# Attention and a 4-bit linear layer on one core: queue points of four loads, a third place for values, two subtractions on another engine, one fill later

## The chip, the cores and the metric

The kernel runs on one core of a Trainium2 chip. The time is what the device takes for one launch, in microseconds (us): a median of separate runs. TensorE (PE) multiplies matrices, VectorE (DVE) and ScalarE (ACT) work element by element, GpSimd (POOL) too, SyncE (SP) only issues DMA transfers, all into one queue. Engines run their own instructions in order and wait for each other by semaphores.

## The reference

```python
x = layernorm(x + attention(x))        # x: 4 x 1024 x 512, f32
x = layernorm(x + linear(x))           # both operands rounded to 4 bits in blocks of 32
# attention: 32 heads of 16
q, k, v = x @ Wq.T, x @ Wk.T, x @ Wv.T
q1, q2 = halves(q); q = concat(q1*cos - q2*sin, q1*sin + q2*cos)   # k likewise (rope)
s = q @ k.T / 4 + bias[i - j]          # bias where 0 <= i - j < 256; masked where i < j
m = max(max_j(s), off);  p = exp(s - m)
out = (p @ v) / (sum_j p + exp(off - m)) @ Wo.T
```

## The kernel before

The work has three stages. Stage one (to about 326 us) makes q, k and v for 4096 tokens in 8 chunks of 512 tokens. Each chunk has four *pairs* (32 in all, numbered by `done` or `n`; b is the batch, eight pairs each). A pair is two 128-row tiles of q or k (the two halves that rope mixes) and one tile of v. f32 operands are split into a high and a low part: ScalarE writes the high part (`weight_hi`, `operand_hi`), VectorE the low part of the weights (L1291), GpSimd the low part of x (`operand_lo`, L1205). TensorE multiplies three products of 512 columns for each of four k-steps (L808).

For a pair, in order: ScalarE copies the two tiles out of PSUM (`take_up`, L980); VectorE multiplies them by the cosines (`by_cosine`, L1384) while GpSimd multiplies the copy by the sines (`turn_by_sine`, L1200); VectorE adds and subtracts (`rotate`, L1396). The result is cut into three bf16 parts: first part on ScalarE (L997), the rest on VectorE (`take_rest`, L1402), second part on ScalarE (`second_part`, L1001), third part on VectorE (`third_part`, L1371). The buffer `rest` is single: the next `take_rest` waits for the third part. SP stores the parts to DRAM (`store_parts`, six transfers), from four buffers, two of them for the last eight pairs. Values go from PSUM to one of two places in `v_sb` (L989), and from there to DRAM (L618); the last eight pairs use one place, since the other receives the first values for stage two.

The rope tables for cosines and sines hold two pieces, for even and odd pairs, and are reloaded by SP once in a chunk each (`load_rope`, L513). After batches 0, 1 and 2 SP also loads back the *stack* of that batch (`load_stack`, L540 and L543, nine transfers of 1.5 MB together): six blocks of q parts beside six of k parts, so that one bf16 matmul gives an accurate product.

From pair 12 on TensorE also computes the row maxima products of the first two batches between its product matmuls (`maxima`, L716), into a ring of three PSUM banks, and VectorE reduces them (`max_unit`, L1306 and L1313) at set places between a pair's steps. TensorE waits when all three banks are full.

Stage two (to about 1425 us) runs 8 groups of heads over 4 batches: scores, exponentials, products with v. Stage three is the output projection, the layer norms and the linear layer. The passage from stage one to stage two is called the seam here: the last pair's parts are made while the first score units run (`u` numbers them; ScalarE's exponentials are L1051), and three maxima units (`seam`) are done by VectorE in it.

SP's order in one step of stage one is: wait for the pair's values and store them; at the second pair of a chunk load the next x; at a chunk's last and first pair load a rope table; store the parts of the pair before; then `loads_beside`, the stack and bias loads. At the very start SP loads Wq and x in quarters (L516, L508), Wv (L519), the rope tables and, once VectorE has split Wq, Wk (L524). GpSimd fills some constants first, among them 3 rows of ones in the stacks (L1185) and the ones beside the values (L1188). ScalarE's first instruction waits for both kinds of fill (`ones_set`).

## Time and profile before

| | |
|---|---|
| runs | 1656.5, 1656.63, 1661.16 us; median 1656.63 |
| the profiled execution | 1662.25 us, span of its instructions 1660.3 us |
| granted TensorE clock, mean | 0.976 |
| busy: PE, DVE, ACT, POOL | 1555.8, 1291.1, 1108.2, 248.7 us |

A clock of 1.00 is 2.4 GHz, 0.50 is 1.2 GHz. "Idle before" in a row is the time that the engine stood still just before the instruction, and the name behind the arrow is what ended it. "issue" there means that the profile shows no releaser.

### The profile page before, as it was taken

The numbers are of one execution on the slowest core, as the hardware profiler recorded it, in microseconds if no ns is written. First come the engines' busy times: TensorE is split into PE (matmuls) and PEld (weight loads), VectorE is DVE, ScalarE is ACT, GpSimd is POOL, SyncE is SP. The second block draws the span as 40 slices with busy tenths as digits, with TensorE's granted clock in tenths as the row PEclk, the third lists the DMA queues.
The fourth block names the chain that finished last, engine by engine and source line by source line (L and its number), as shares of the span: only waits on it lengthen the run. The fifth ranks groups of instructions, "written<-read, shape, count | busy, mean of one in ns | idle before, by whom it ended". The sixth has DMA issues, their size and how long they took to land. (4 is left out here: it accounts for less than half of the span.)

```text
span 1660.3 us, 28811 instructions
## 1 busy us (share of the span) xinstructions
PE 1555.8 (94%) x9552; PEld 816.4 (49%) x9552; DVE 1291.1 (78%) x3830; ACT 1108.2 (67%) x1620; POOL 248.7 (15%) x157
## 2 busy tenths in 40 slices
PE   7999989789999999999999999999999998899984
PEld 5876657544444444444444444444444443444431
DVE  5567878678888888888888888878888876289995
ACT  4543434467787878878788787887778888434542
POOL 5544434200000000000000000000000000033442
PEclk9999999989999999999999999999999999999995
DMA  5595656534433334432542434433353202013221
GB/s 196 174 240 173 161 165 176 155 78 94 74 55 80 52 60 73 90 46 47 107 69 46 81 55 73 89 57 47 59 110 54 46 9 85 26 51 102 77 77 51
DMA packets 129257, 147.59 MB, mean 89 GB/s; under 512 B 48595, under 2 KB 81427, under 8 KB 129110
## 3 DMA queue, kind: packets, MB, share of 16 engines
q1 hardware_dynamic: 129110, 145.76, 39.4%
q8 instruction: 77, 1.26, 0.3%
q14 instruction: 70, 0.57, 0.1%
HBM read 102.32 MB, written 42.60 MB: 87 GB/s over the span
## 5 line engine op out<-in xcount | busy, mean ns | idle before, releaser
L1051 ACT ACTIVATE probs<-ps 128x1024 f32<-128x1024 f32 (+3 forms) x768 | 592.2, 810 | 181.5 <-PE ps L743 120.4
L1313 DVE CUSTOM_DVE_ANT_0 junk<-ps,bias_q 128x384 bf16<-128x384 f32 (+2 forms) x1024 | 502.7, 502 | 149.1 <-PE ps L716 135.3
L716 PE MATMUL ps<-k_stack,q_stack 96*128 96x384 bf16 (+3 forms) x1536 | 494.1, 335 | 24.0 <-DVE mx L1306 11.8
L737 PE MATMUL ps<-q_stack,k_stack 99*128 99x512 bf16 (+3 forms) x1536 | 490.5, 329 | 15.6 <-ACT ps L1066 5.3
L1306 DVE TENSOR_REDUCE mx<-ps 128x1 f32<-128x128 f32 (+3 forms) x768 | 365.3, 485 | 47.6 <-PE ps L716 40.6
L743 PE MATMUL ps<-bias_r,ident_r 128*128 128x384 f32 (+2 forms) x1280 | 352.7, 363 | 0.0
L716 PEld LDWEIGHTS ps<-k_stack,q_stack 96*128 96x128 bf16 x1536 | 143.0, 97 | 374.3 <-DVE mx L1313 149.2
L758 PE MATMUL ps<-probs,v_sb 128*17 128x512 f32 (+3 forms) x3072 | 323.2, 493 | 0.1
L808 PE MATMUL ps<-split 128*128 128x512 f32 x1152 | 291.3, 411 | 18.0 <-POOL split L1205 12.4
L808 PEld LDWEIGHTS ps<-split 128*128 128x128 f32 x1152 | 221.2, 195 | 60.5 <-POOL split L1205 12.4
L743 PEld LDWEIGHTS ps<-bias_r,ident_r 128*128 128x128 f32 x1280 | 223.2, 193 | 37.0 <-issue 0.4
L1066 ACT ACTIVATE ps<-bias_s 128x768 f32<-128x768 f32 (+2 forms) x320 | 197.0, 616 | 23.2 <-ACT probs L1051 1.2
L737 PEld LDWEIGHTS ps<-q_stack,k_stack 99*128 99x128 bf16 x1536 | 147.3, 99 | 98.6 <-issue 45.0
L1214 POOL CAST bias_r<-work 128x768 fp32r<-128x768 f32 x8 | 7.5, 936 | 847.9 <-DMA work<-ext_k_dram 847.9
L927 PE MATMUL ps<-q_stack,k_stack 128*128 128x512 f32 x256 | 117.4, 605 | 6.5 <-ACT k_stack L1118 6.5
L758 PEld LDWEIGHTS ps<-probs,v_sb 128*17 128x17 f32 x3072 | 51.2, 95 | 118.5 <-issue 96.8
L1200 POOL TENSOR_TENSOR probs<-probs,o_sb 128x1024 f32<-128x1024 f32 x30 | 73.1, 2436 | 127.5 <-ACT probs L980 73.7
L1313 DVE DVE_READ_ACCUMULATOR2_ANT mx<- 128x1 f32 x1024 | 84.5, 83 | 0.0
L1064 ACT ACTIVATE ps<-zero 128x256 f32<-128x256 f32 (+2 forms) x128 | 70.0, 547 | 14.8 <-ACT probs L1051 0.4
L927 PEld LDWEIGHTS ps<-q_stack,k_stack 128*128 128x128 f32 x256 | 48.1, 193 | 58.6 <-issue 48.8
L1396 DVE TENSOR_TENSOR probs<-probs 128x512 f32<-128x512 f32 x60 | 43.5, 766 | 20.2 <-POOL probs L1200 20.2
L1259 POOL TENSOR_TENSOR probs<-k_stack,qinv 128x1024 f32<-128x1024 f32 x16 | 30.6, 1912 | 128.2 <-DVE qinv L1475 128.2
(122 smaller groups left out, 1103.0 us busy)
## 6 DMA issues: line engine op xcount, KB each, us to landing
q_stack<-q_parts SPq DMA_DIRECT2D x192, 128.0 KB, 4.3
k_stack<-k_parts SPq DMA_DIRECT2D x32, 384.0 KB, 7.1
q_parts<-q_stack SPq DMA_DIRECT2D x84, 128.0 KB, 2.1
k_parts<-k_stack SPq DMA_DIRECT2D x84, 128.0 KB, 2.0
v_dram<-v_sb SPq DMA_DIRECT2D x32, 272.0 KB, 2.1
v_sb<-v_dram SPq DMA_DIRECT2D x32, 272.0 KB, 8.8
k_stack<-k_parts SPq DMA_DIRECT2D x32, 256.0 KB, 7.8
q_stack<-h SPq DMA_DIRECT2D x16, 512.0 KB, 4.1
```

The lines of the kernel that those rows point to most:

```text
L716: pe.matmul(ps_ring[:, use.bank, 0:c1 - c0], q_stack[0:STACK, b, hl, I * P:(I + 1) * P], k_stack[0:STACK, b, hl, c0:c1], start=True, stop= ...
L737: mm = pe.matmul(ps_s[:, u % 2, hh, 0:w], k_stack[0:ROWS, b, hl, J * P:(J + 1) * P], q_stack[0:ROWS, b, hl, i0:i0 + w], start=not in_bank, ...
L743: mm = pe.matmul(ps_s[:, u % 2, hh, 0:bw], ident_r[:, :], rhs, start=False, stop=(s == 1))
L758: mm = pe.matmul(ps_o[VW * hl:VW * hl + VS, i0 - CH * c:CH], v_in[:, b % 2, J, VS * hl:VS * (hl + 1)], probs[:, T % 3, hl, 0:w], start=(J ...
L808: mm = pe.matmul(ps[:, RING + tile % PBANKS, :], lhsT, rhs, start=(kt == 0 and first + second == 0), stop=(kt == NK - 1 and first == 1))
L927: mm = pe.matmul(ps_y[t % 3], at_T[par][:, w, kt * P:(kt + 1) * P], wo_sb[:, kt, :], start=(kt == 0), stop=(kt == NK - 1))
L1051: act.activation(probs[:, (u // 2) % 3, 2 * pr:2 * pr + 2, 0:w], ps_s[:, pr, :, 0:w], ACT.Exp).then_inc(exp_done, 1)
L1064: act.activation(ps_s[:, 1, :, bw:w], zero[:, :].unsqueeze(2).broadcast_to([P, 2, w - bw]), ACT.Copy)
L1066: act.activation(ps_s[:, 1:2, :, 0:bw], bias_s[:, bass.ds(g % 2, 1), :, b0:b0 + bw], ACT.Copy)\
L1200: pool.tensor_tensor(turned, turned, rope_sin[q % 2].unsqueeze(1).broadcast_to([P, 2, CH]), ALU.mult).then_inc(sin_ready, 1)
L1306: ins = dve.tensor_reduce(mx[:, par, hl, I, slot:slot + 1], ps_ring[:, use.bank, 0:far], AX.X, ALU.max)
L1313: ins = dve.tensor_tensor_reduce(out=junk[:, use.bank, 0:c1 - lo], in0=ps_ring[:, use.bank, lo - c0:c1 - c0], in1=bias_q[:, hl, BAND - t0 ...
```

## The change

Five edits, all in stage one or at its end:

1. GpSimd's fill of the ones rows in the stacks moves from its start to behind its first four low parts of x. ScalarE no longer waits for any fill before its first copy; it waits for the two small fills of the value places before the first `take_up`.
2. SP loads a rope table ahead of the step's value store, no longer behind it.
3. The stacks of batches 1 and 2 are loaded one step of the queue earlier: after the parts of pairs 16 and 24 are stored, no longer after those of pairs 17 and 25. The first load of the row shifts moves one step later, behind the parts of pair 25.
4. `v_sb` holds three places: two for values on their way out through all 32 pairs, and one that receives the first values for stage two. The first load of those waits only for batch 0's stores.
5. The third parts of pairs 30 and 31 are made by GpSimd. VectorE's `take_rest` of pair 31 now waits for GpSimd's third part of pair 30; ScalarE makes pair 31's second part after the second exponential, no longer after the third.

```diff
 def v_turn(pair):
-    def slot(pair):
-        return pair % 2 if pair < PAIRS - 8 else 1
-    return slot(pair), sum(slot(x) == slot(pair) for x in range(pair))
+    return pair % 2, pair // 2
...
-        v_kept = v_sb[:, :, :, :].rearrange("p r j w -> p r (j w)")[:, :, 0:NB * HG * VS]
-        v_in = v_kept.rearrange("p r (j w) -> p r j w", j=NB)
-        v_out = v_kept.rearrange("p r (h w) -> p r h w", w=VS)
+        v_flat = v_sb[:, :, :, :].rearrange("p r j w -> p (r j w)")
+        v_places = [v_flat[:, i * NB * HG * VS:(i + 1) * NB * HG * VS] for i in range(3)]
+        v_in = [v_places[i].rearrange("p (j w) -> p j w", j=NB) for i in (0, 2)]
+        v_out = [v_places[i].rearrange("p (h w) -> p h w", w=VS) for i in (1, 2)]
...
                 if (b, q) == (1, 1):
-                    sp.wait_ge(ones_set, 1)
+                    sp.wait_ge(ones_set, 3)
...
-                if (b, q) == (2, 2):
+                if (b, q) == (2, 1):
                     wait_parts(16)
                     load_stack(0, 1, 1)
-                if (b, q) == (3, 2):
+                if (b, q) == (3, 1):
                     wait_parts(24)
                     load_stack(0, 2, 2)
                 if (b, q) == (3, 4):
-                    sp.wait_ge(v_stored[0], FIRST + 16 * v_uses(24)[0])
-                    sp.wait_ge(v_stored[1], FIRST + 16 * v_uses(8)[1])
+                    for i in range(2):
+                        sp.wait_ge(v_stored[i], FIRST + 16 * v_uses(8)[i])
                     load_v(0, 0, 0)
-                if (b, q) == (3, 1):
+                if (b, q) == (3, 2):
                     load_shift(0, 0)
             for b in range(B):
                 for pair in range(8):
                     c, q = pair // 4, pair % 4
+                    chunk, done = 2 * b + c, 8 * b + pair
+                    if q == 3 and chunk < 2 * B - 1 or q == 0 and chunk:
+                        sp.wait_ge(raw_read_dve, FIRST + done)
+                        sp.wait_ge(sin_ready, FIRST + done)
+                        load_rope((c + 1) % 2 if q == 3 else c, (done - 1) % 2)
                     slot = v_turn(8 * b + pair)[0]
                     wait_then_address(v_ready, FIRST + b * 8 + pair + 1)
...
-                        .rearrange("p (h w) -> p h w", w=VS), v_out[:, slot]).then_inc(v_stored[slot], 16)
-                    chunk, done = 2 * b + c, 8 * b + pair
+                        .rearrange("p (h w) -> p h w", w=VS), v_out[slot]).then_inc(v_stored[slot], 16)
                     if q == 1 and chunk < 2 * B - 1:
                         sp.wait_ge(hT_lo, NK * (chunk + 1))
                         for kt in range(NK):
                             load_hT(chunk + 1, kt)
-                    if q == 3 and chunk < 2 * B - 1 or q == 0 and chunk:
-                        sp.wait_ge(raw_read_dve, FIRST + done)
-                        sp.wait_ge(sin_ready, FIRST + done)
-                        load_rope((c + 1) % 2 if q == 3 else c, (done - 1) % 2)
                     if b or pair:
                         store_parts(8 * b + pair - 1)
...
-            act.wait_ge(ones_set, 3)
             def weight_hi(w, kt):
...
             for w in (2, 1):
                 for kt in range(NK):
                     weight_hi(w, kt)
+            act.wait_ge(ones_set, 2)
             for done in range(PAIRS):
...
-                        if n == 0 and u == 2:
-                            second_part(PAIRS - 1)
...
                         seed_after(g, n, u, (g,) if b < B - 1 else () if last else (g + 1,))
+                        if n == 0 and u == 1:
+                            second_part(PAIRS - 1)
...
             pool.wait_ge(ident_ready, 2)
-            pool.memset(k_stack[STACK:ROWS, 0:2, :, :], 1.0).then_inc(ones_set, 1)
-            pool.wait_ge(ones_set, 1)
             for r in range(2):
-                pool.memset(v_out[:, r, :, D:VS], 1.0).then_inc(ones_set, 1)
+                pool.memset(v_out[r][:, :, D:VS], 1.0).then_inc(ones_set, 1)
...
             for kt in range(NK):
                 operand_lo(0, kt)
+            pool.wait_ge(hT_lo, NK)
+            pool.memset(k_stack[STACK:ROWS, 0:2, :, :], 1.0).then_inc(ones_set, 1)
+            pool.wait_ge(ones_set, 3)
             for b in range(B):
                 for pair in range(8):
                     turn_by_sine(b, pair)
...
+            for n in (PAIRS - 2, PAIRS - 1):
+                pool.wait_ge(rot_ready, FIRST + 2 * PAIRS)
+                pool.wait_ge(rot_mid, n + 1)
+                buf = part_turn(n)[0]
+                pool.tensor_tensor(part_bufs[buf][:, 2, :, :], rest, part_bufs[buf][:, 1, :, :],
+                                   ALU.subtract).then_inc(rot_lo, 1)
             pool.wait_ge(sin_ready, FIRST + 32)
...
                 maximum(n + 1, 1)
-                if n:
+                if n and not last:
                     third_part(n - 1)
                 if last:
                     dve.wait_ge(v_ready, FIRST + 32)
                     seam(0)
+                    dve.wait_ge(rot_lo, PAIRS - 1)
...
             for k in range(1, SEAM):
                 seam(k)
-            third_part(PAIRS - 1)
```

On GpSimd, at the start of the program (`split` is the high and low parts, `k_stack 3x8192` the ones rows, `v_sb 128x32` the ones beside the values), before:

```order
L1185 MEMSET k_stack 3x8192 [waits ident_ready]
L1188 MEMSET v_sb 128x32 [waits ones_set]
L1188 MEMSET v_sb 128x32
L1189 MEMSET mx 128x192
L1190 MEMSET eps 128x1
L1191 MEMSET zero 128x2
L1192 CAST ident_r<-ident 128x128
L1205 TENSOR_TENSOR split<-q_stack,split 128x512 [waits hT_hi]
L1205 TENSOR_TENSOR split<-k_stack,split 128x512 [waits hT_hi]
L1205 TENSOR_TENSOR split<-work,split 128x512 [waits hT_hi]
L1205 TENSOR_TENSOR split<-hT_in,split 128x512 [waits hT_hi]
L1200 TENSOR_TENSOR probs<-probs,o_sb 128x1024 [waits rope_loaded0,raw_ready]
```

and in the changed kernel:

```order
L1185 MEMSET v_sb 128x32 [waits ident_ready]
L1185 MEMSET v_sb 128x32
L1186 MEMSET mx 128x192
L1187 MEMSET eps 128x1
L1188 MEMSET zero 128x2
L1189 CAST ident_r<-ident 128x128
L1202 TENSOR_TENSOR split<-q_stack,split 128x512 [waits hT_hi]
L1202 TENSOR_TENSOR split<-k_stack,split 128x512 [waits hT_hi]
L1202 TENSOR_TENSOR split<-work,split 128x512 [waits hT_hi]
L1202 TENSOR_TENSOR split<-hT_in,split 128x512 [waits hT_hi]
L1221 MEMSET k_stack 3x8192 [waits hT_lo]
L1197 TENSOR_TENSOR probs<-probs,o_sb 128x1024 [waits rope_loaded0,raw_ready,ones_set]
```

The long fill now stands behind the two short ones and the four low parts, and ahead of the first sine step.

On SP, from the steps of pairs 17 to 19 (`q_parts<-q_stack` stores parts; `q_stack<-q_parts` and `k_stack<-k_parts` load the stack; `v_dram<-v_sb` stores values; `rope_tables` and `o_sb` are the cosines and sines), before:

```order
L618 DMA v_dram<-v_sb 128x544 [waits v_ready]
L579 DMA q_parts<-q_stack 128x512 [waits rot_lo]
L579 DMA q_parts<-q_stack 128x512 x5
L540 DMA q_stack<-q_parts 16x4x1024 [waits parts_stored2,parts_stored3,parts_stored1,parts_stored0]
L540 DMA q_stack<-q_parts 16x4x1024 x5
L543 DMA k_stack<-k_parts 48x4x1024
L543 DMA k_stack<-k_parts 32x4x1024
L543 DMA k_stack<-k_parts 16x4x1024
L618 DMA v_dram<-v_sb 128x544 [waits v_ready]
L513 DMA rope_tables<-cos 128x512 [waits sin_ready,raw_read_dve]
L513 DMA o_sb<-sin 128x512
```

and in the changed kernel:

```order
L540 DMA q_stack<-q_parts 16x4x1024 [waits parts_stored2,parts_stored3,parts_stored1,parts_stored0]
L540 DMA q_stack<-q_parts 16x4x1024 x5
L543 DMA k_stack<-k_parts 48x4x1024
L543 DMA k_stack<-k_parts 32x4x1024
L543 DMA k_stack<-k_parts 16x4x1024
L624 DMA v_dram<-v_sb 128x544 [waits v_ready]
L579 DMA q_parts<-q_stack 128x512 [waits rot_lo]
L579 DMA q_parts<-q_stack 128x512 x5
L513 DMA rope_tables<-cos 128x512 [waits sin_ready,raw_read_dve]
L513 DMA o_sb<-sin 128x512
L624 DMA v_dram<-v_sb 128x544 [waits v_ready]
```

The nine transfers of the stack now precede pair 18's values and pair 17's parts, and the tables precede pair 19's values.

On VectorE, from the last rotation on (`q_stack<-probs,q_stack` and `k_stack<-probs,k_stack` are the third parts of pairs 30 and 31, `probs<-attn,k_stack` is the rest of pair 31, L1313, L1320, L1306 reduce maxima), before:

```order
L1396 TENSOR_TENSOR attn<-attn 128x512
L1371 TENSOR_TENSOR q_stack<-probs,q_stack 128x1024 [waits rot_mid]
L1313 ISA junk,mx<-ps,bias_q 128x128 [waits bias_q_loaded0,ring_filled,rot_lo,v_ready]
L1313 ISA mx 128x1
L1402 TENSOR_TENSOR probs<-attn,k_stack 128x1024 [waits rot_hi,rot_ready]
L1313 ISA junk,mx<-ps,bias_q 128x256 [waits ring_filled]
L1313 ISA mx 128x1
L1313 ISA junk,mx<-ps,bias_q 128x384 [waits ring_filled]
L1313 ISA mx 128x1
L1371 TENSOR_TENSOR k_stack<-probs,k_stack 128x1024 [waits rot_mid]
L1306 TENSOR_REDUCE mx<-ps 128x1 [waits ring_filled,sin_ready,rot_lo]
```

and in the changed kernel:

```order
L1403 TENSOR_TENSOR attn<-attn 128x512
L1320 ISA junk,mx<-ps,bias_q 128x128 [waits bias_q_loaded0,v_ready,ring_filled]
L1320 ISA mx 128x1
L1409 TENSOR_TENSOR probs<-attn,k_stack 128x1024 [waits rot_hi,rot_ready,rot_lo]
L1320 ISA junk,mx<-ps,bias_q 128x256 [waits ring_filled]
L1320 ISA mx 128x1
L1320 ISA junk,mx<-ps,bias_q 128x384 [waits ring_filled]
L1320 ISA mx 128x1
L1313 TENSOR_REDUCE mx<-ps 128x1 [waits ring_filled,sin_ready]
```

Both third parts are gone from VectorE, and the rest of pair 31 waits for `rot_lo`, which counts the third parts.

## Rows read from the trace of the kernel before

**Rows 1.** Stretches: us; busy of PE, PEld, DVE, ACT, POOL; granted clock; DMA.
```profile
137.00:164.00 27.00, 25.59 (x108) 19.00 (x109) 20.48 (x39) 12.44 (x16) 10.90 (x7) 0.94 0.46 149
164.00:201.00 37.00, 33.28 (x148) 24.11 (x147) 34.81 (x55) 14.36 (x19) 19.83 (x11) 1.00 0.54 163
201.00:240.00 39.00, 31.61 (x128) 22.74 (x127) 30.64 (x51) 12.87 (x15) 8.94 (x6) 0.91 0.65 172
292.00:304.00 12.00, 7.07 (x20) 5.00 (x19) 7.35 (x14) 2.12 (x3) 2.34 (x1) 0.72 0.76 231
326.00:345.00 19.00, 11.29 (x44) 5.30 (x44) 12.06 (x33) 9.32 (x15) 4.12 (x2) 0.64 0.29 99
345.00:1500.00 1155.00, 1129.54 (x7809) 535.46 (x7808) 912.66 (x3159) 894.56 (x1337) 42.71 (x34) 1.00 0.36 65
```

**Rows 2.** Timeline, the start: start us, length us, instruction, [idle, releaser].
```profile
2.62 6.92 POOL L1185 MEMSET k_stack<- 3x8192 bf16 x1
...
3.97 1.28 ACT L1011 ACT_TABLE_LOAD   x1 [3.97 <-DMA q_stack<-wqT]
...
5.00 0.66 SPq L519 DMA_DIRECT2D q_stack<-wvT  x1
...
9.84 0.63 ACT L1011 ACTIVATE split<-q_stack 128x512 fp32r<-128x512 f32 x1 [4.59 <-POOL v_sb L1188]
...
11.54 8.24 DVE L1291 SCALAR_TENSOR_TENSOR split<-q_stack,split 128x512 fp32r<-128x512 f32 x7 [0.35 <-ACT split L1011]
...
12.40 27.83 PE L808 MATMUL ps<-split 128*128 128x512 f32 x112 [12.40 <-POOL split L1205]
...
16.31 0.38 SPq L524 DMA_DIRECT2D q_stack<-wkT  x1
...
22.36 2.50 DVE L1291 SCALAR_TENSOR_TENSOR split<-q_stack,split 128x512 fp32r<-128x512 f32 x4 [2.58 <-ACT split L1011]
```

**Rows 3.** DMA issues of the first 20 us: count, KB, us to landing.
```profile
q_stack<-wvT SPq DMA_DIRECT2D x1, 1024.0 KB, 7.8
...
q_stack<-wkT SPq DMA_DIRECT2D x1, 1024.0 KB, 5.4
...
o_sb<-sin SPq DMA_DIRECT2D x2, 256.0 KB, 8.0
```

**Rows 4.** TensorE's product matmuls, 12 to 13.5 us, then 50 to 60 us.
```profile
L808 PE MATMUL ps<-split 128*128 128x512 f32 x3 | 1.6, 685 | 12.4 <-POOL split L1205 12.4
...
L808 PE MATMUL ps<-split 128*128 128x512 f32 x45 | 10.4, 390 | 0.0
```

**Rows 5.** Timeline, GpSimd's sine steps that wait for a sine table.
```profile
127.15 2.40 POOL L1200 TENSOR_TENSOR probs<-probs,o_sb 128x1024 f32<-128x1024 f32 x1 [9.99 <-DMA o_sb<-sin]
...
211.54 2.36 POOL L1200 TENSOR_TENSOR probs<-probs,o_sb 128x1024 f32<-128x1024 f32 x1 [10.14 <-DMA o_sb<-sin]
...
295.51 2.34 POOL L1200 TENSOR_TENSOR probs<-probs,o_sb 128x1024 f32<-128x1024 f32 x1 [10.11 <-DMA o_sb<-sin]
```

**Rows 6.** The sine load issued at 202.48 us, and at 159.09 us.
```profile
o_sb<-sin SPq DMA_DIRECT2D x1, 256.0 KB, 8.9
...
o_sb<-sin SPq DMA_DIRECT2D x1, 256.0 KB, 4.0
```

**Rows 7.** Timeline, DMA issues (SPq) around the stack load.
```profile
183.10 3.22 SPq L579 DMA_DIRECT2D q_parts<-q_stack  x6
...
197.39 2.67 SPq L540 DMA_DIRECT2D q_stack<-q_parts  x6
```

**Rows 8.** Timeline, VectorE: the rest of pair 18.
```profile
183.71 3.32 DVE L1402 TENSOR_TENSOR probs<-probs,q_stack 128x1024 f32<-128x1024 f32 x1
```

**Rows 9.** Timeline, the seam of the first two stages.
```profile
335.72 1.05 ACT L1001 ACTIVATE k_stack<-probs 128x1024 bf16<-128x1024 f32 x1
...
336.80 1.23 DVE L1371 TENSOR_TENSOR k_stack<-probs,k_stack 128x1024 bf16<-128x1024 f32 x1 [4.02 <-ACT k_stack L1001]
...
338.88 0.50 PE L716 MATMUL ps<-k_stack,q_stack 96*128 96x384 bf16 x1 [3.90 <-DVE mx L1313]
```

More of the change, by code:

```diff
@@ L546, in load_v @@
             def load_v(g, b, buf):
-                sp.dma_start(v_in[:, buf, :, :],
+                sp.dma_start(v_in[buf],
                              v_dram[b * S:(b + 1) * S, bass.ds(g * HG * VS, HG * VS)]
@@ L988, in take_values @@
                 act.wait_ge(v_stored[slot], FIRST + 16 * turn)
-                act.activation(v_out[:, slot, :, 0:D],
+                act.activation(v_out[slot][:, :, 0:D],
                                ps[:, RING + (3 * n + 2) % PBANKS, :].rearrange("p (h d) -> p h d", d=D), ACT.Copy)\
```

2 lines of the change are left out of this document (1 added, 1 removed).

## The prediction

> **What bounds the kernel now.** I read the busy shares first, then cut the run into stages. TensorE is busy 94% of the span, VectorE 78%. In the middle stage TensorE is busy 1129.5 of 1155 us at full clock (the last of [rows 1]). The change touches nothing there, so every microsecond must come from stage one or the seam. There TensorE loses time in three ways, and the reader should see each in [rows 1]: idle time (length minus the first busy number), the clock (at 0.91 over 39 us the work of 0.09 x 39 us is missing), and the start, where it first works at 12.40 us [rows 2]. Then I asked the timeline what released each idle engine. At the start it is GpSimd's fill; three times it is a sine table that comes 10 us late [rows 5]; in the seam it is VectorE behind a third part [rows 9].
>
> **The start.** ScalarE's first copy runs at 9.84 us after 4.59 us of idle, released by GpSimd's small fill, which stands behind the 6.92 us fill of the ones rows [rows 2]. With the long fill moved, the first copy waits only for its data, which are there at 3.97 us; the table load of 1.28 us may even come before them. That frees 4.59 to 5.9 us. What is late next is the data. TensorE's third tile needs the low parts of Wv. Wv is issued at 5.00 us and lands 7.8 us later [rows 3], at 12.8. Four copies of 0.63 us and one split of 2.50/4 = 0.63 us follow [rows 2]: 15.9 us. Before, these splits ended at 11.54 + 8.24 = 19.8 us. The gain there is 3.9 us. Wk is next: its issue (16.31 us) follows the first splits and comes forward, but behind the sine tables, which land 8.0 us after their issue near 7 us, at 15.4; with a transfer's 5.4 us less the part that overlaps it lands at about 18 to 19, before at 21.7, so 3 us or more earlier. TensorE needs it only after six further tiles. Its first matmuls are slow (685 against 390 ns, [rows 4]): that slow piece moves along with the start and costs the same, or a little less, as some of it now falls into waiting for x. I take **4.3 us**, bounds 3.0 and 5.3. The long fill now ends near 13 + 6.9 = 20 us, before the first sine step has its data (ScalarE's copy stands behind the Wk copies, not before 20 us): no cost. If that cover failed, a late fill would hold only the sine step, by under 1 us.
>
> **The tables and the stacks.** The sine load issued at 202.48 us needed 8.9 us; the same load without a stack ahead of it needed 4.0 [rows 6]. The stack was issued from 197.39 us; the parts that now precede it were out at 183.10 + 3.22 = 186.3 us [rows 7]. So the stack starts 11 us earlier, and it was 8.9 us of queue. The table's own wait (both uses of the old table done) is met when the parts of the pair before are stored, so it goes out where the stack began, at 197.4 us, no longer 5 us later behind the stack's nine issues and a value store. It should land near 201.5 to 203.5 instead of 211.5, where GpSimd was ready at 211.54 - 10.14 = 201.4. Of 10.1 us of waiting 8 or more go; the same for the third late table at 295.51. What they cost TensorE: in 201 to 240 us it idles 39 - 31.6 = 7.4 us and loses up to 3.5 us by the clock; I count 3.0 of these, as some of the slow time is idle, together 10.4. The stage from 164 to 201 us has the same work and no late table, idles 3.7 us and keeps its clock [rows 1]. So 10.4 - 3.7 = **6.7 us** go, bounds 3 and 10. In 292 to 304 us: 4.9 idle and 3.4 by the clock, counted 3.0, less 12/37 of 3.7 = 1.2: **6.7 us**, bounds 3 and 8. The first late table (127.15 us) stands behind a stack that does not move; it gains only its 272 KB value store and half a microsecond of issue, some 1.5 us of 10. In 137 to 164 us TensorE loses 1.4 + 0.06 x 27 = 3.0 us; I take half, **1.5 us**, bounds 0 and 3. The four earlier chunks have no maxima, and TensorE is fully busy there whatever its helpers wait for: nothing. The shifts, moved one step later, are needed only at the seam, 40 us on: nothing, and if late, one transfer.
>
> The value store now stands behind the table's wait, and pair 18's behind nine stack issues. Behind it wait ScalarE's values two pairs later, 18 us on (37/4 = 9.25 us a pair in 164 to 201 us): nothing. The second place for the last eight pairs makes that true there as well; with one place it would have been the next thing late. I cost it at nothing in itself, bounds 0 and 1 us gained.
>
> **The seam.** Pair 31's second part is written at 335.72 us, only then VectorE's third part at 336.80, and TensorE stands 3.90 us for a ring bank that VectorE frees behind it [rows 9]. In the new order VectorE does not stop there. Against it: the rest of pair 31 waits for GpSimd's third part of pair 30. No row shows that subtraction on GpSimd. The nearest, its 128x1024 multiply, takes 2.40 us [rows 5], VectorE's third part 1.23 [rows 9]; I take 2.4, the upper bound being twice this. So the rest starts some 0.9 us later, since VectorE had one third part to do itself in that time. 3.9 - 0.9 = **3.0 us**, bounds -1 and 6 (with some of the 0.36 x 19 us that the clock takes there).
>
> The Trainium skill, GPSIMD Engine Reference, section Engine selection, says that an elementwise step with two inputs belongs on VectorE, being about twice as slow on GpSimd. The rows agree (2.40 against 1.23). By that rule alone the edit loses 2.4 us and the sum falls by 5.4; I go by the wait that it removes.
>
> **Sum.** 4.3 + 1.5 + 6.7 + 6.7 + 3.0 = 22.2 us. The profiled execution took 1662.25 us (span 1660.3), which gives 1640.1. It was 5.6 us above the median of the runs, and 1656.63 - 22.2 = 1634.4. Part of that 5.6 us may be just such slow-clock pieces as I subtract, so I take the middle: **1637 us**.
>
> **Rivals.** *VectorE takes the place of the table.* It is busy 34.8 of 37 us in 164 to 201 us [rows 1], the rest of pair 18 takes 3.32 us there, beside a GpSimd multiply [rows 8], against 1.23 us for a VectorE step of the same size [rows 9]. When the sine steps come in time, more VectorE steps run beside one and stretch by up to 2 us each, and the ring fills again. For it: 94% busy. Against it: over 201 to 240 us VectorE is busy only 30.6 of 39. Half of the three middle terms is lost, 7.5 us: 1645.
>
> Of this the Trainium skill, SBUF — State Buffer, section Who interferes with whom, says that a VectorE instruction with two SBUF inputs and a GpSimd instruction that reads SBUF exclude each other for a whole instruction. The 3.32 us row agrees. By it the moved third parts also hold VectorE's rest, which here waits for them anyway.
>
> *The waiting only moves.* The queue stays full (parts, values, stack, tables in a row), the table still comes late, and only start and seam remain: 7.3 us, 1652 by the same middle.
>
> *Slower.* The last eight pairs have two part buffers. In the new order the stack of batch 2 lies ahead of pair 25's parts, and pair 27's first part waits for their landing, about one pair (9.25 us) after their issue. A transfer right behind a stack needed 8.9 us [rows 6]. If they need more than 9.25 us, ScalarE, VectorE and the ring stop: 10 us as in [rows 5] plus 3 by the clock. With the middle terms gone that is 13 - 7.3 = +5.7: 1662 on the median. Against it: these parts are issued some 4 us behind the stack, not at once.
>
> *More than forecast.* The ring never fills again and the seam keeps its clock: 3.7 + 1.2 + 1.5 + 4 us more: 1627.
>
> **Chances.** Forecast 0.52 (own range 1631 to 1644), VectorE 0.24, moved waits 0.10, more 0.08, slower 0.06. About 0.3% (5 us) is what a measurement of this kernel can tell from no change. Faster: 0.52 + 0.24 + 0.08 and 0.04 of the moved waits, 0.88; the other 0.06 of these are the same; slower 0.06. The range, 1628 to 1651, leaves out half of the large gain, half of the moved waits and the slower case, 0.15.
>
> **What would show it.** TensorE's first matmul at 7 to 8 us, ScalarE's first copy near 4 to 5. GpSimd's sine steps of pairs 20 and 28 with under 2 us of DMA wait, that of pair 12 still with 8. No half-clock piece in the 40 us after pair 20. No third part on VectorE at the seam and no 3.9 us stop. Stage two starts 19 us earlier (the first four terms), at about 307 us against 326 now. I am wrong if rests of 3 us multiply while TensorE waits for maxima, if a first part waits for a part store, or if the start moves under 3 us.

## The result and the profile after

The changed kernel took 1637.94 us (median of 4 runs, 1634.76 to 1640.08), the kernel before beside it 1658.32 (median of 4). The ratio is 0.9874, 95% interval 0.9848 to 0.99: faster by 20.4 us. The profiled execution took 1639.82 us, span 1637.9, mean granted clock 0.983 (before 0.976). Marks below are read from such single executions: the one before lay 3.9 us above its kernel's median, this one 1.9 us above, so the two traces differ by 22.4 us where the medians differ by 20.4.

The stretches as in [rows 1]; the columns are the same. The fourth and fifth are the end of stage one and the seam, which now lie earlier:

```profile
137.00:164.00 27.00, 26.18 (x118) 19.10 (x116) 21.94 (x38) 10.77 (x14) 18.90 (x10) 1.00 0.52 166
164.00:201.00 37.00, 34.17 (x146) 24.81 (x145) 33.56 (x54) 16.43 (x21) 16.15 (x9) 0.95 0.75 192
201.00:240.00 39.00, 38.71 (x174) 28.63 (x173) 33.73 (x70) 16.55 (x21) 16.66 (x9) 1.00 0.52 165
285.00:304.00 19.00, 17.36 (x79) 12.63 (x77) 14.43 (x27) 7.34 (x9) 4.17 (x3) 1.00 0.42 135
304.00:323.00 19.00, 15.01 (x93) 7.13 (x93) 15.34 (x50) 12.06 (x19) 8.58 (x4) 0.82 0.41 121
325.00:1480.00 1155.00, 1127.61 (x7761) 532.98 (x7755) 910.72 (x3136) 893.90 (x1329) 43.18 (x34) 1.00 0.36 64
```

TensorE is busy 38.71 of 39 us at full clock in the third, before 31.61 at 0.91. The stretch ahead of it still idles 2.8 us. TensorE stands 2.24 us of that at 181.00 us, for a VectorE instruction (L1396) that follows the 3.32 us rest of pair 18; the kernel before has the same wait (2.23 us at 188.4). After it the granted clock is 0.83 from 180 to 190 us, and so 0.95 in the stretch, before 1.00.

The timeline of the start, as in [rows 2]:

```profile
3.96 0.63 ACT L1009 ACTIVATE split<-q_stack 128x512 fp32r<-128x512 f32 x1 [1.46 <-DMA q_stack<-wqT]
...
7.02 2.21 PEld L808 LDWEIGHTS ps<-split 128*128 128x128 f32 x6 [7.02 <-POOL split L1202]
...
12.13 0.38 SPq L524 DMA_DIRECT2D q_stack<-wkT  x1
```

The first copy comes at 3.96 us, before 9.84, and TensorE starts at 7.02, before 12.40. Wk is issued 4.2 us earlier. The landings as in [rows 3], where the last column is the time from issue to landing, show that the loads now lie closer together and each takes a little longer (Wv 8.1 us and Wk 6.9, before 7.8 and 5.4):

```profile
q_stack<-wvT SPq DMA_DIRECT2D x1, 1024.0 KB, 8.1
...
q_stack<-wkT SPq DMA_DIRECT2D x1, 1024.0 KB, 6.9
```

GpSimd's sine steps of pairs 12, 20 and 28, as in [rows 5], and SP's issues of the stack and of the sine table of pair 20, as in [rows 7]:

```profile
121.45 2.40 POOL L1197 TENSOR_TENSOR probs<-probs,o_sb 128x1024 f32<-128x1024 f32 x1 [8.75 <-DMA o_sb<-sin]
...
198.28 2.92 POOL L1197 TENSOR_TENSOR probs<-probs,o_sb 128x1024 f32<-128x1024 f32 x1 [3.49 <-ACT probs L980]
...
272.34 2.39 POOL L1197 TENSOR_TENSOR probs<-probs,o_sb 128x1024 f32<-128x1024 f32 x1 [3.54 <-ACT probs L983]
```

```profile
178.67 2.68 SPq L540 DMA_DIRECT2D q_stack<-q_parts  x6
...
190.72 0.46 SPq L513 DMA_DIRECT2D o_sb<-sin  x1
```

The second and third step now wait for ScalarE's copy and no longer for a DMA, so 3.5 us of their 10.1 us were never the table's; the first still waits 8.75 us. The sine table of pair 20 goes out 12.0 us behind the stack's first issue, before 202.48 - 197.39 = 5.1 us, and landed 5.0 us later.

TensorE's first two waits in the seam before, which [rows 9] does not have:

```profile
330.88 0.53 PE L716 MATMUL ps<-k_stack,q_stack 96*128 96x512 bf16 x1 [2.03 <-DVE mx L1313]
...
332.45 0.37 PE L774 MATMUL ps<-ident,shift 128*32 128x128 f32 x1 [1.04 <-DVE mx L1313]
```

The timeline of the seam in the changed kernel, as in [rows 9]:

```profile
306.38 2.12 POOL L1245 TENSOR_TENSOR q_stack<-probs,q_stack 128x1024 bf16<-128x1024 f32 x1 [1.56 <-DVE attn L1403]
...
306.57 0.39 PE L716 MATMUL ps<-k_stack,q_stack 96*128 96x512 bf16 x1 [0.59 <-DVE mx L1320]
...
308.54 1.23 DVE L1409 TENSOR_TENSOR probs<-attn,k_stack 128x1024 f32<-128x1024 f32 x1 [2.02 <-POOL q_stack L1245]
...
310.25 0.37 PE L774 MATMUL ps<-ident,shift 128*32 128x128 f32 x1 [3.29 <-DVE mx L1320]
...
310.99 2.13 POOL L1245 TENSOR_TENSOR k_stack<-probs,k_stack 128x1024 bf16<-128x1024 f32 x1 [2.49 <-ACT k_stack L1001]
```

GpSimd's third part takes 2.12 us. VectorE waits 2.02 us for it, TensorE, in front of the shift matmul, stands 3.29 us for VectorE behind that (before 1.04 us), and the stop of 3.90 us is gone. The window from the first score to the first copy, before (326.74 to 351.03 us) and in the changed kernel:

```profile
326.74:351.03 24.29, 17.21 (x93) 7.99 (x94) 17.07 (x52) 12.37 (x19) 4.46 (x2) 0.72 0.46 115
```

```profile
303.86:323.19 19.33, 15.34 (x93) 7.35 (x94) 15.67 (x50) 12.39 (x20) 8.72 (x4) 0.82 0.42 121
```

TensorE idles 3.99 us of it, before 7.08, and 93 matmul records in both take 15.34 us at a clock of 0.82, before 17.21 at 0.72.

Where the time went is read best from marks that all traces have. The table gives their times in us from the span's start; "19 to 23" is the way from the sine step of pair 19 to that of pair 23, "first score" the first L737 matmul, "first copy" the first copy of a result to `o_sb`, "step" one batch of one group in stage two (32 of them):

| kernel | pair 10 | pair 19 | 19 to 23 | first score | seam to first copy | step | last copy |
|---|---|---|---|---|---|---|---|
| before | 103.03 | 199.01 | 46.43 | 326.74 | 24.29 | 34.26 | 1425.30 |
| changed | 98.56 | 192.37 | 37.38 | 303.86 | 19.33 | 34.45 | 1403.07 |
| the same again | 98.68 | 191.40 | 36.49 | 302.00 | 18.71 | 34.45 | 1400.54 |
| edit 1 alone | 98.33 | 192.62 | 46.27 | 320.14 | 24.27 | 34.26 | 1418.68 |
| edit 2 alone | 103.30 | 196.66 | 45.76 | 323.82 | 24.35 | 34.26 | 1422.42 |
| edit 3 alone | 102.56 | 197.80 | 37.31 | 309.23 | 23.45 | 34.26 | 1406.93 |
| edit 5 alone | 103.79 | 199.50 | 44.41 | 325.10 | 19.24 | 34.45 | 1424.24 |
| edits 1 to 4 | 98.52 | 192.40 | 37.35 | 303.87 | 24.51 | 34.26 | 1402.56 |
| 1 to 4, ScalarE's order | 98.42 | 191.73 | 37.04 | 302.91 | 20.31 | 34.26 | 1397.55 |
| changed, padded | 98.95 | 192.47 | 37.23 | 303.81 | 18.73 | 34.26 | 1396.83 |

Two traces of the same kernel differ by 1.9 us at the first score, so single marks say little below 2 us; much of it fits the clock, which is 0.83 from 180 to 190 us in the first and 1.00 in the second (0.17 x 10 = 1.7 us). The step, which repeats within a trace to 0.03 us in 28 of its 31 values, says much more. From before to the changed kernel, stage one gained 22.88 us and the seam 4.96, together 27.84 at the first copy. At the last copy 22.23 are left: stage two gave 5.6 us back, 0.18 or 0.19 in each batch step.

### The profile page after: what moved, and what is told of

It reads as the page before. It is cut to its first block and busy times, and to the rows that moved or that the text cites. A ratio compares the mean times of both kernels' runs of the same rounds, so it can differ in the third digit from the quotient of the medians.

```text
span 1637.9 us, 28803 instructions
## 1 busy us (share of the span) xinstructions
PE 1550.1 (95%) x9542; PEld 810.6 (49%) x9552; DVE 1289.1 (79%) x3828; ACT 1112.0 (68%) x1620; POOL 257.3 (16%) x159
## 5 line engine op out<-in xcount | busy, mean ns | idle before, releaser
L1320 DVE CUSTOM_DVE_ANT_0 junk<-ps,bias_q 128x384 bf16<-128x384 f32 (+2 forms) x1024 | 503.0, 503 | 147.3 <-PE ps L716 133.7
L737 PE MATMUL ps<-q_stack,k_stack 99*128 99x512 bf16 (+3 forms) x1536 | 491.7, 328 | 12.5 <-ACT ps L1065 4.9
L1313 DVE TENSOR_REDUCE mx<-ps 128x1 f32<-128x128 f32 (+3 forms) x768 | 365.3, 485 | 45.7 <-PE ps L716 38.7
L808 PE MATMUL ps<-split 128*128 128x512 f32 x1152 | 285.6, 406 | 9.7 <-POOL split L1202 7.0
L808 PEld LDWEIGHTS ps<-split 128*128 128x128 f32 x1152 | 216.7, 191 | 52.2 <-POOL split L1202 7.9
L737 PEld LDWEIGHTS ps<-q_stack,k_stack 99*128 99x128 bf16 x1536 | 147.0, 98 | 95.9 <-issue 42.1
L1320 DVE DVE_READ_ACCUMULATOR2_ANT mx<- 128x1 f32 x1024 | 84.7, 83 | 0.0
```

Source lines behind the costliest of these rows:

```text
L737: mm = pe.matmul(ps_s[:, u % 2, hh, 0:w], k_stack[0:ROWS, b, hl, J * P:(J + 1) * P], q_stack[0:ROWS, b, hl, i0:i0 + w], start=not in_bank, ...
L808: mm = pe.matmul(ps[:, RING + tile % PBANKS, :], lhsT, rhs, start=(kt == 0 and first + second == 0), stop=(kt == NK - 1 and first == 1))
L1313: ins = dve.tensor_reduce(mx[:, par, hl, I, slot:slot + 1], ps_ring[:, use.bank, 0:far], AX.X, ALU.max)
L1320: ins = dve.tensor_tensor_reduce(out=junk[:, use.bank, 0:c1 - lo], in0=ps_ring[:, use.bank, lo - c0:c1 - c0], in1=bias_q[:, hl, BAND - t0 ...
```

## The experiments

The intervals are those of the ratio to the kernel before, timed on the same chip.

**The edits one by one.** Edit 1 alone:

```diff
-                    sp.wait_ge(ones_set, 1)
+                    sp.wait_ge(ones_set, 3)
...
-            act.wait_ge(ones_set, 3)
...
                     weight_hi(w, kt)
+            act.wait_ge(ones_set, 2)
...
-            pool.memset(k_stack[STACK:ROWS, 0:2, :, :], 1.0).then_inc(ones_set, 1)
-            pool.wait_ge(ones_set, 1)
...
                 operand_lo(0, kt)
+            pool.wait_ge(hT_lo, NK)
+            pool.memset(k_stack[STACK:ROWS, 0:2, :, :], 1.0).then_inc(ones_set, 1)
+            pool.wait_ge(ones_set, 3)
```

> Only the fill moved (edit 1). Theory: ScalarE's first copy near 4.0 us, TensorE's first matmul near 7.0 us, and every mark of stage one 4.4 to 4.5 us earlier than before (pair 10's sine step at about 98.6 us, before 103.03), kept to the end: 1653 to 1654 us. Rival: the gain is swallowed by the late tables or by the seam, because VectorE is what sets the pace of chunks 3 to 7: marks from pair 12 on less than 2 us earlier, 1656 to 1658 us.

1654.13 us, 0.997 (0.9955 to 0.9984). The trace is 4.7 us ahead at pair 10 and 6.6 at the first score, of which up to 2 are the scatter of traces; the medians differ by 4.1 us. The start is worth what its term said.

Edit 3 alone:

```diff
-                if (b, q) == (2, 2):
+                if (b, q) == (2, 1):
                     wait_parts(16)
...
-                if (b, q) == (3, 2):
+                if (b, q) == (3, 1):
                     wait_parts(24)
...
-                if (b, q) == (3, 1):
+                if (b, q) == (3, 2):
                     load_shift(0, 0)
```

> Only the stacks of batches 1 and 2 one step earlier and the shift load one step later (edit 3). Theory: this edit alone brings the tables of pairs 20 and 28 in time; marks 8 to 9 us earlier at pair 23 and 13 to 15 us at the first score: 1642 to 1645 us. Rival A: the tables also need their own earlier place ahead of the values (edit 2), without it half is left: 1648 to 1651 us. Rival B: with one place for the last values ScalarE waits for the store of pair 27's values and the gain at pair 28 is lost: 8 to 9 us only, 1648 to 1650 us, to be told from A by the sine wait of pair 20 (A: several us, B: under 1 us).

1645.33 us, 0.9915 (0.9902 to 0.9929). The way from pair 19 to 23 is 37.31 us, as in the changed kernel: this edit alone takes the late tables of pairs 20 and 28 away and brings 17.5 us at the first score, the most of all (12.9 us between the medians, 0.3 us outside the expected range). A new late table appears, that of pair 29, but it costs next to nothing. The timeline of SP and GpSimd there:

```profile
282.84 0.32 SPq L618 DMA_DIRECT2D v_dram<-v_sb  x1
...
283.69 0.44 SPq L513 DMA_DIRECT2D o_sb<-sin  x1
...
287.63 2.96 POOL L1200 TENSOR_TENSOR probs<-probs,o_sb 128x1024 f32<-128x1024 f32 x1 [7.53 <-DMA o_sb<-sin]
```

The sine table is issued behind the value store, which waited for its values until 282.84 us, and GpSimd's idle time of 7.53 us ends with its landing. In the changed kernel GpSimd idles 7.24 us ahead of the same step, for ScalarE's copy, so the table is some 0.3 us late; from the sine step of pair 28 to the first score both kernels need the same (277.70 to 309.23 and 272.34 to 303.86, 31.5 us).

Edit 2 alone:

```diff
+                    if q == 3 and chunk < 2 * B - 1 or q == 0 and chunk:
+                        sp.wait_ge(raw_read_dve, FIRST + done)
+                        sp.wait_ge(sin_ready, FIRST + done)
+                        load_rope((c + 1) % 2 if q == 3 else c, (done - 1) % 2)
                     slot = v_turn(8 * b + pair)[0]
                     wait_then_address(v_ready, FIRST + b * 8 + pair + 1)
...
-                    if q == 3 and chunk < 2 * B - 1 or q == 0 and chunk:
...
-                        load_rope((c + 1) % 2 if q == 3 else c, (done - 1) % 2)
```

> Only the tables ahead of the value stores (edit 2). Theory: they still stand behind the stacks and gain one value store of queue and under 1 us of issue each: sine waits of pairs 12, 20 and 28 of 8.5 to 9.5 us, before 10; 0 to 3 us of time, 1654 to 1658 us. Rival: the queue position is what counts, and half of the middle gain comes from it: sine waits under 5 us, 1648 to 1652 us.

1656.42 us, 0.9985 (0.9975 to 0.9995). With the stack where it was, its nine transfers still stand ahead of the tables: pairs 12, 20 and 28 wait 8.11, 9.37 and 10.13 us. It brings 2.9 us at the first score, 1.8 between the medians.

Edit 5 alone (cut to the lines that place it; "..." marks what is left out):

```diff
-                        if n == 0 and u == 2:
-                            second_part(PAIRS - 1)
...
                         seed_after(g, n, u, (g,) if b < B - 1 else () if last else (g + 1,))
+                        if n == 0 and u == 1:
+                            second_part(PAIRS - 1)
...
+            for n in (PAIRS - 2, PAIRS - 1):
...
+                pool.tensor_tensor(part_bufs[buf][:, 2, :, :], rest, part_bufs[buf][:, 1, :, :],
+                                   ALU.subtract).then_inc(rot_lo, 1)
...
-                if n:
+                if n and not last:
                     third_part(n - 1)
...
+                    dve.wait_ge(rot_lo, PAIRS - 1)
...
-            third_part(PAIRS - 1)
```

> Only the last two third parts on GpSimd, with ScalarE's second part one unit earlier (edit 5). Theory: no mark before the first score moves (326.7 us), the first copy of the output accumulator comes 4 to 5.5 us earlier than before (351.0): 1652 to 1654 us. Rival: the seam's gain in the changed kernel came from its stage one arriving in better order, and alone the edit gives 0 to 2 us: 1656 to 1658 us.

1659.48 us, 1.0003 (0.9992 to 1.0014). Neither expected total came. The seam is 5.05 us shorter and the kernel no faster: each batch step takes 34.45 us.

**The change without edit 5**, so edits 1 to 4:

```diff
+                        if n == 0 and u == 2:
+                            second_part(PAIRS - 1)
...
-                        if n == 0 and u == 1:
-                            second_part(PAIRS - 1)
...
-            for n in (PAIRS - 2, PAIRS - 1):
...
-                if n and not last:
+                if n:
                     third_part(n - 1)
...
-                    dve.wait_ge(rot_lo, PAIRS - 1)
...
+            third_part(PAIRS - 1)
```

> The change without its seam edit (edits 1 to 4). Marks of stage one as in the changed kernel: first score near 304 us, 22 to 24 us earlier than before. The first copy of the output accumulator then 47 to 48 us... that is near 328 us, 5 us later than the changed kernel's 323.2, since the seam is as before. In stage two the step per batch is 34.26 us in the kernels that keep the old seam and 34.45 in those with the new one. Theory P (the seam edit puts stage two into the slower step): 34.26 us here, 5.6 us back over stage two, 1636 to 1640 us, no different from the changed kernel within 2 us. Rival Q (the slower step belongs to the earlier start of stage two or to the values' new places): 34.45 us, 1641 to 1645 us.

1638.42 us, 0.9873 (0.9859 to 0.9887), the same as the changed kernel. VectorE and TensorE at the old stop:

```profile
313.93 1.23 DVE L1370 TENSOR_TENSOR k_stack<-probs,k_stack 128x1024 bf16<-128x1024 f32 x1 [4.02 <-ACT k_stack L999]
...
316.01 0.50 PE L714 MATMUL ps<-k_stack,q_stack 96*128 96x384 bf16 x1 [3.90 <-DVE mx L1312]
```

The 3.90 us are back in the seam, and the step is 34.26 us. One pays for the other. By the medians edits 1, 2 and 3 alone bring 4.1, 1.8 and 12.9 us, 18.8 in sum, and edits 1 to 4 together 20.6 (1658.99 to 1638.42), so they stand beside each other within a few us.

**Only ScalarE's order.** Edits 1 to 4, and of edit 5 only this; both third parts stay on VectorE:

```diff
-                        if n == 0 and u == 2:
-                            second_part(PAIRS - 1)
                         seed_after(g, n, u, (g,) if b < B - 1 else () if last else (g + 1,))
+                        if n == 0 and u == 1:
+                            second_part(PAIRS - 1)
```

> Edits 1 to 4, and of the seam edit only ScalarE's part: pair 31's second part after the second exponential; both third parts stay on VectorE. Theory: what cost 3.9 us was ScalarE's second part standing behind the third exponential, and the subtraction itself (1.2 us) never mattered; VectorE no longer waits for GpSimd's third part of pair 30, so the seam gains as much as in the changed kernel or 1 us more: first copy of the accumulator 322 to 324 us. Rival: VectorE, with the third part behind three maxima units, still holds the ring, and half of the gain is lost: 325 to 327 us. On stage two's step: if GpSimd's part in the seam edit makes the slower step, 34.26 us and 1631 to 1634 us; if it is the moment at which stage two starts, 34.45 may come here too, 1636 to 1640 us.

1633.68 us, 0.9846 (0.9832 to 0.9859), 4.3 us below the changed kernel's median and 3.7 below the same kernel timed on the same chip (1637.41, the next experiment); the runs of the two do not overlap (1633.12 to 1634.36, and 1635.53 to 1640.15). TensorE's waits in this seam:

```profile
307.05 0.39 PE L714 MATMUL ps<-k_stack,q_stack 96*128 96x512 bf16 x1 [2.03 <-DVE mx L1312]
...
308.62 0.27 PE L772 MATMUL ps<-ident,shift 128*32 128x128 f32 x1 [1.18 <-DVE mx L1312]
...
311.37 0.50 PE L714 MATMUL ps<-k_stack,q_stack 96*128 96x384 bf16 x1 [1.14 <-DVE mx L1312]
```

The three stops are 2.03, 1.18 and 1.14 us. So the long stop went with ScalarE's earlier second part alone, and GpSimd was not needed for it.

**The changed kernel once more**, with no edit:

> The changed kernel once more, nothing altered. If the step of stage two is fixed by the kernel: 34.45 us per batch in this execution too, marks of stage one within 2 us of the first profile, 1636 to 1640 us. If it is drawn anew in each execution: 34.26 us is possible, and then about 1634 us.

1637.41 us, 0.987 (0.9854 to 0.9886), step 34.45 us.

**The table of pair 12.** The changed kernel with the loads of `bias_q` 1 to 3 and of `bias_k` behind pair 12's tables:

```diff
-                    for hl in range(HG):
-                        load_bias_q(0, hl)
-                    load_bias_k(0)
+                    load_bias_q(0, 0)
+                if (b, q) == (1, 4):
+                    load_bias_q(0, 1)
+                    load_bias_q(0, 2)
+                if (b, q) == (1, 5):
+                    load_bias_q(0, 3)
+                    load_bias_k(0)
```

> The changed kernel, with three of four bias transfers and the bias for the scores (1.4 MB of the 3 MB issued at pair 9's step) put behind the tables of pairs 12 and 13. Theory: the sine wait of pair 12 falls from 8.75 us to 2 to 4, and with it half of what TensorE still loses from 120 to 165 us: marks from pair 15 on 1 to 3 us earlier, 1635 to 1638 us. Rival: TensorE is not held by that wait (its ring stall there was 0.94 us), 0 to 1 us.

1636.55 us, 0.9864 (0.9849 to 0.9879). Pair 12's wait for DMA is gone (its step starts at 117.42 us, in the changed kernel 121.45), but the first score comes at 300.98 us against 302.00 and 303.86 in the two traces without this edit. Not told apart from nothing: TensorE stood only 0.94 us there (ahead of its matmul at 132.7 us), and two traces without this edit have their first score at 300.82 and 301.39 us.

The same edit on the faster version (edits 1 to 4, ScalarE's order):

> Edits 1 to 4 and ScalarE's reorder of edit 5, both third parts on VectorE as before, and the loads of bias_q 1 to 3 and bias_k behind pair 12's rope tables. Theory (the effects of the bias move and of leaving the third parts on VectorE stand beside each other): the sine step of pair 12 does not wait, stage two's step is 34.26 us, median 1631 to 1633. Rival (the bias move only fills a gap that the ring makes up): median 1633.5 to 1635, although pair 12's wait is gone.

1632.51 us, 0.9839 (0.9824 to 0.9855), step 34.26 us. Both kernels are beaten, the one before by 1.6%; the median is the lowest of all, by 0.02 us, and its interval overlaps those of its neighbours, and so what the bias loads give stays open.

**Why the step is longer.** The changed kernel with VectorE's `neg_off` computed three times and not once, at pair 11: two tiny instructions, so that VectorE has as many ahead of stage two as before.

```diff
-                    dve.wait_ge(neg_off_ready, 1)
+                    for i in (1, 2):
+                        dve.wait_ge(neg_off_ready, i)
+                        dve.tensor_scalar(neg_off[:, :], off[:, :], -1.0, None, ALU.mult).then_inc(neg_off_ready, 1)
+                    dve.wait_ge(neg_off_ready, 3)
```

> The changed kernel, with two tiny VectorE instructions (neg_off computed twice more, at pair 11) so that VectorE has as many instructions ahead of stage two as before the change. Theory A (the 0.19 us that each batch step of stage two takes longer hangs on where VectorE's instructions lie in its stream, two instructions earlier since both third parts left it): the step is 34.26 us again, median 1631 to 1633. Rival B (it hangs on GpSimd's part in the seam, or on the moment and order in which stage two is entered): the step stays 34.45 us, median 1636 to 1638.

1633.75 us, 0.9846 (0.9831 to 0.9861); the step is 34.26 us, as theory A has it, and the whole is 0.75 us above its range. GpSimd still makes the third parts here, so it wasn't GpSimd. The waits of TensorE from 400 to 1400 us, with the total in us, their count and the longest, in the changed kernel:

```profile
PE ps L737 <- ACT ps L1065: 4.9, 7, 1.1
PE ps L716 <- DVE mx L1320: 2.9, 19, 0.2
PE ps L737 <- ACT probs L1050: 0.7, 2, 0.3
```

The same view of the padded kernel:

```profile
PE ps L735 <- ACT ps L1064: 5.0, 8, 1.1
PE ps L914 <- issue: 1.1, 1, 1.1
PE ps L765 <- ACT o_sb L1076: 0.7, 1, 0.7
PE ps L735 <- ACT probs L1049: 0.7, 2, 0.3
```

The changed kernel waits 19 times, up to 0.2 us, for VectorE's maxima (L1320), the padded one never; the three other kernels with the long step wait so 24 or 25 times, the kernel before never. One such place in the timeline of the kernel before:

```profile
590.44 0.69 DVE L1306 TENSOR_REDUCE mx<-ps 128x1 f32<-128x512 f32 x1
...
590.85 0.73 PE L716 MATMUL ps<-k_stack,q_stack 96*128 96x512 bf16 x2
...
591.05 0.55 DVE L1313 CUSTOM_DVE_ANT_0 junk<-ps,bias_q 128x384 bf16<-128x384 f32 x1
...
591.66 0.10 PEld L716 LDWEIGHTS ps<-k_stack,q_stack 96*128 96x128 bf16 x1 [0.36 <-DVE mx L1313]
```

The same place in the changed kernel:

```profile
563.90 0.69 DVE L1313 TENSOR_REDUCE mx<-ps 128x1 f32<-128x512 f32 x1
...
564.31 0.73 PE L716 MATMUL ps<-k_stack,q_stack 96*128 96x512 bf16 x2
...
564.81 0.56 DVE L1320 CUSTOM_DVE_ANT_0 junk<-ps,bias_q 128x384 bf16<-128x384 f32 x1 [0.21 <-PE ps L716]
...
565.43 0.10 PEld L716 LDWEIGHTS ps<-k_stack,q_stack 96*128 96x128 bf16 x1 [0.67 <-DVE mx L1320]
```

And in the padded one:

```profile
561.95 0.69 DVE L1311 TENSOR_REDUCE mx<-ps 128x1 f32<-128x512 f32 x1
...
562.36 0.74 PE L714 MATMUL ps<-k_stack,q_stack 96*128 96x512 bf16 x2
...
562.56 0.55 DVE L1318 CUSTOM_DVE_ANT_0 junk<-ps,bias_q 128x384 bf16<-128x384 f32 x1
```

In the first and the last, VectorE's masked maximum (L1313, L1318 padded) starts 0.61 us after its reduction (590.44 to 591.05). In the changed kernel the same instruction starts 0.91 us after it. TensorE's matmuls start 0.41 us after the reduction in all three, so a late matmul isn't the cause, though the row names one as releaser. The next matmul of the maxima comes 0.81 us after the first pair of them before (590.85 to 591.66) and 1.12 in the changed kernel, released by VectorE.

The same two instructions on the version with ScalarE's order alone:

> Edits 1 to 4 and ScalarE's reorder, third parts on VectorE, with the same two tiny VectorE instructions, so that its stream is two longer than before. Theory A (place in the stream): the step leaves 34.26 us if the places repeat every four instructions, 34.45 and 1638 to 1640; with a longer repeat it may stay. Rival B (GpSimd's part or the entry): 34.26 us, median 1633 to 1635.

1632.53 us, 0.9838 (0.9819 to 0.9856), step 34.26 us. Two instructions too many do no harm, two too few do. So the places don't repeat every four. But in this stream, too, one instruction is late. The reduction and the masked maximum one round ahead of those above, first in the padded version, then in the kernel before:

```profile
592.87 0.55 DVE L1305 TENSOR_REDUCE mx<-ps 128x1 f32<-128x384 f32 x1
...
593.50 0.56 DVE L1312 CUSTOM_DVE_ANT_0 junk<-ps,bias_q 128x384 bf16<-128x384 f32 x1
```

```profile
589.43 0.55 DVE L1306 TENSOR_REDUCE mx<-ps 128x1 f32<-128x384 f32 x1
...
589.90 0.55 DVE L1313 CUSTOM_DVE_ANT_0 junk<-ps,bias_q 128x384 bf16<-128x384 f32 x1
```

The maximum starts 0.63 us after its reduction, before 0.47, and so in every step. The step does not show it. Which place in the stream this is, is told at the end.

**The value places.** Edits 1 to 3 and ScalarE's order, the values with one place in the last eight pairs:

```diff
-    return pair % 2, pair // 2
+    def slot(pair):
+        return pair % 2 if pair < PAIRS - 8 else 1
+    return slot(pair), sum(slot(x) == slot(pair) for x in range(pair))
...
-                    for i in range(2):
-                        sp.wait_ge(v_stored[i], FIRST + 16 * v_uses(8)[i])
+                    sp.wait_ge(v_stored[0], FIRST + 16 * v_uses(24)[0])
+                    sp.wait_ge(v_stored[1], FIRST + 16 * v_uses(8)[1])
```

> Edits 1 to 3 and ScalarE's reorder, third parts on VectorE; the values keep one place for the last eight pairs (edit 4 left out). Theory (the value places were worth nothing in themselves, and the late table of pair 29 with the stack edit alone came from its place behind the values' store): no sine step of pairs 20 to 31 waits more than 2 us for a table, median 1633 to 1635. Rival (with one place ScalarE's value copy waits for a store that now stands behind table and stack): ScalarE waits for DMA at one of pairs 25 to 29, the ring fills, TensorE stops, median 1637 to 1643.

1634.39 us, 0.9848 (0.9832 to 0.9863), no different from the version with edit 4. No sine step behind pair 12 waits for a table. SP near pair 29:

```profile
273.29 0.45 SPq L513 DMA_DIRECT2D o_sb<-sin  x1
...
275.01 0.33 SPq L623 DMA_DIRECT2D v_dram<-v_sb  x1
```

The sine table now goes out 1.7 us ahead of the value store. So the order of edit 2 is enough to keep the table of pair 29 in time; edit 4 was worth nothing that shows.

## Why the prediction was right, and where it was right by luck

The time was right (1637 against 1637.94), and so was the account of what bounds stage one. The profiled execution agrees too: 1640.1 forecast, 1639.82 measured. But the sum was 22.2 us and the two stages in which I summed gained 27.84; the term that was missing, stage two, took 5.6 of these back. That the rest is 22.2 again is luck: what the terms fell short by and what was left out are equal by chance.

- *The start*, 4.3: right. 4.47 us at pair 10, and 4.7 with edit 1 alone.
- *The first table*, 1.5: about right. A further 2.2 us by pair 19, with 8.75 of 9.99 us of its wait still there; moving that wait away bought nothing measurable.
- *201 to 240 us*, 6.7: too small. 9.05 us went between pairs 19 and 23. I had let the 3.7 us of the stretch ahead stand as a floor. It was none: 2.2 us of them is the one wait behind pair 18's stretched rest, and TensorE idles 0.29 us in the later stretch now. The clock was counted rightly as part of the loss, and is 1.00 there. Of the 10.1 us of the table's wait I took 8 or more as the table's; 6.65 were, since 3.49 us stay as a wait for ScalarE's copy.
- *292 to 304 us*, 6.7: right. From pair 27 to the first score 6.28 us, and another 0.9 between pairs 23 and 27 which I had put at nothing.
- *The value places*, nothing: right, by the last experiment. That they would have been late next was wrong.
- *The seam*, 3.0: too small, 4.96 us, though the waits came as summed. TensorE's idle time fell from 7.08 to 3.99 us, by 3.09: the stop of 3.90 went, and the two stops ahead of it grew from 3.07 to 3.88 us, near the 0.9 that I charged for GpSimd's slower step. The other 1.87 us are the same matmuls in less time, at a clock of 0.82 for 0.72; I had left the clock to the bounds. What was put wrongly is the cause: I reckoned edit 5 as one piece. ScalarE's order alone shortens this way by 4.2 us (24.51 to 20.31), and with the third parts on GpSimd it is 18.7 to 19.3 us in five traces, on VectorE 19.1 to 20.3 in four. What GpSimd adds can't be told from nothing. The step took 2.12 us, for which I had 2.4. The Trainium skill, GPSIMD Engine Reference, section Engine selection, has it about twice as slow as VectorE; 2.12 against 1.23 is 1.7 times. Its advice to leave such a step on VectorE is neither borne out nor refuted by the time: with stage two's step at 34.26 us the version on GpSimd took 1633.75 us, those on VectorE 1633.68 and 1632.53.
- *Stage two*, not in the sum: "the change touches nothing there" failed. True of its code, not of where VectorE's code lies. It cost 5.6 us.

Of the rivals, *VectorE takes the place* did not come where it was put: in 201 to 240 us VectorE is busy 33.73 us and TensorE 38.71, and the two rests of over 3 us that the kernel before has there are gone. But its mechanism came once, beside the sine step of pair 28. That runs from 272.34 us, a rest beside it takes 3.32 us from 272.49, and TensorE then waits for a maximum, where the stretch from 260 to 285 us had no idle time before:

```profile
277.66 0.39 PE L716 MATMUL ps<-k_stack,q_stack 96*128 96x512 bf16 x1 [1.43 <-DVE mx L1313]
```

That is 1.4 us of idle time; the rests of over 3 us did not multiply (five in stage one, before six). *The waiting only moves* happened once, at pair 29, only without edit 2, and by 0.3 us. *Slower* did not come: ScalarE never waits for a part store. *More than forecast* was true of stage one and the seam in size, not in its conditions: the ring still fills in the seam, and the clock there is 0.82.

## What to carry to other kernels

Take late transfers off the queue by moving the long one ahead of them to a point where it can start earlier; moving the short one within its step brought a sixth of that at the first score. Test each half of an edit apart: here a reorder of one ScalarE instruction did the work that was credited to moving two others to GpSimd. Ask of a late transfer what its engine would have waited for without it: of 10.1 us 3.5 stayed, and of 7.5 us 7.2. And where the gain of a stage is not in the total, compare the period of the stages behind it to 0.02 us, also those whose code is the same.

## What the runs showed of the hardware

**The number of VectorE instructions ahead of a stretch changed its speed.** All four traces of kernels with two VectorE instructions fewer ahead of stage two (the changed one twice, edit 5 alone, the changed one with the later bias loads) have a step of 34.45 us, the ten others, two of them padded, 34.26. Unpadded, GpSimd's part and the shorter VectorE code go together; the padded kernel parts them, and the time follows the code. In the traces each batch step but the last two has exactly 128 VectorE instructions, its waits included, so that a place in the code that is a multiple of some power of two falls on the same instruction in all steps; the late one of the rows above stands 64 places beyond a multiple of 128 in the changed kernel's stream, 66 before and padded, 68 in the padded version of ScalarE's order.

In that last stream another masked maximum stands 64 beyond, and it is the one that starts 0.63 us after its reduction, in all steps from 450 to 1350 us, where the thirteen other traces have 0.47. So it is the place that is late, whichever maximum stands there: by 0.28 us in the mean in the changed kernel, which the step shows, and by 0.17 us here, which it does not. The plain reduction that stands there before and padded starts 0.07 us after the instruction ahead of it, as it does on place 62 in the changed kernel; so not every instruction is late there. No run shows what delays it.

The Trainium skill, Runtime: NRT & Kernel Launch, section Instruction fetch mechanics, says that an engine's instruction memory is refilled in blocks of 256 instructions and that crossing one is mostly hidden. By that rule a late instruction would come in every second step at most. The trace shows the slip in every one, so the rule as it stands does not explain it. What stays open is which other places are bad (only 0, 2 and 4 instructions on from the changed kernel's were run) and why.

**A tiny cast waited for GpSimd.** In the changed kernel's seam, beside GpSimd's subtraction of 310.99 us, VectorE's second cast of the shifts took 1.41 us. The timeline of it before:

```profile
339.36 0.21 DVE L1346 CAST shift_parts<-shift_rest 32x128 bf16<-32x128 f32 x1
```

And in the changed kernel:

```profile
311.79 1.41 DVE L1353 CAST shift_parts<-shift_rest 32x128 bf16<-32x128 f32 x1
```

The Trainium skill, SBUF — State Buffer, section Who interferes with whom, names casts among the instructions that can take the port pair shared with GpSimd, and says that whichever of the two was issued first holds it for its whole instruction while the other stands. The trace agrees: the cast ends at 313.20 us, where GpSimd's subtraction ends at 313.12, and it takes 1.40 or 1.41 us in all five traces with the third parts on GpSimd and 0.21 or 0.22 in the nine others. It is one more price of a step on GpSimd that no row before shows.
